# An expert product over two PSUM banks, and the first group's modes copied straight from SBUF to SBUF

## The chip, the cores and the metric

The kernel runs on one core of one Trainium2 chip. The metric is the device time of one execution in microseconds (us). The engines are TensorE (PE, its weight loads shown apart as PEld), VectorE (DVE), ScalarE (ACT), GpSimd (POOL) and SyncE (SP); SP and ACT also issue DMA transfers, shown as SPq and ACTq.

## The reference

The model is a Fourier neural operator over 32 images of 64x64 pixels, followed by one windowed attention and one mixture of experts. Cut to what matters here:

```python
# four layers; x is [B, 32, 64, 64], M1 = M2 = 20 modes kept
x_ft = jnp.fft.rfft2(x, norm='ortho')
out = jnp.einsum('bixy,ioxy->boxy', x_ft[:, :, :M1, :M2], w)   # per mode: 32 -> 32 channels
x1 = jnp.fft.irfft2(out_ft, s=(H, W), norm='ortho')            # back to pixels
x2 = jnp.einsum('bchw,oc->bohw', x, cw) + cb                   # pointwise
x = gelu(x1 + x2)
# ... fc1, gelu, fc2, attention over 65 tokens, and then the experts (64 of them, 6 chosen):
scores = softmax(top_logits)
xW = jnp.einsum('bsd,bskde->bske', x, lattice_weights[indices])
lattice_out = jnp.einsum('bske,bsk->bse', xW, scores)
```

## The kernel before, in words

**The layers.** The 32 images go in two passes of 16 (`GIMG`), each through four layers, so there are eight layers in all. A layer (`layer` in the PE part) has these steps. `forward`: a DFT over columns and rows; ACT copies its result (L1265) into `SPEC`, whose last axis holds 32 numbers per mode: real or imaginary part, and the image of the group and the group. `mix` (L1099 and L1107): per mode a product with the spectral weights; ACT copies the result from PSUM to `MIXED` in seven jobs (L1274, `mix_ready` counts them). `MIXED` has images and parts on partitions; the inverse needs modes on partitions, so the data must cross partitions, and that is done by DMA. `pointwise` (L1147, in layer 0 L1143), then `keep_busy(3)` (L1185), three dummy matmuls that stand ahead of the first inverse. `inverse_rows` (L1124) for group n = 0 to 3 of four images and half y = 0, 1, reading `MODE[n % 2]`; DVE transposes its result (L1367); `inverse_columns` (L1156) adds to the pointwise result in PSUM; ACT applies the Gelu (L1284).

**How the modes reach `MODE`.** For groups 1 to 3 SP stores 400 KB per group from `MIXED` into a DRAM scratch (`spec_scr`, L956), waits until it has landed, and loads it back in two transfers (`load_modes`, L940). For group 0, whose modes are wanted first, SP stores the first four of five column blocks d (80 KB each, L947) as soon as the mix job that holds them is done, waits for the four to land, loads them in two transfers (L940), and then waits for the whole mix. The fifth block goes by four direct copies from `MIXED` to `MODE[0]` of 20 KB each (`straight`, L277), two issued by SP behind those loads, two by ACT as soon as the seventh mix job is done. Only then does SP issue the three stores of groups 1 to 3. PE's first `inverse_rows` waits for the loads and for the four direct copies. In the first layer of the second pass SP waits, between the stores and the loads, until the hidden rows of the pass before have left (`ho_out`, their DMAs are L992), because `HO` shares memory with `MODE[0]`; ACT has the same wait ahead of its copies.

**The expert stage** (the tail, `tail_tensor` and `tail_vector`). The 2080 tokens go in five blocks z of 416 (`ZT`), and in each block over 64 experts, two to a step (32 steps `PAIRS` a block, n runs to 160). PE broadcasts the scores of step n over the partitions (`broadcast`, L443, bf16, into PSUM bank n % 4); DVE multiplies that bank by the tokens `YT` into `ZX` (L887); PE multiplies by the expert weights (`expert_products`, L453, two matmuls of 64 columns side by side for two values of n). PE's order is: broadcasts n and n+1, products n-4 and n-3. Broadcast n waits until DVE has freed its bank (product n-4). In between, at fixed steps, DVE adds the output projection (L870, steps `ADD_AT`), centres eight images (L704 to L706, `CENTRE_AT`) and finishes them (L711 to L880, `FINISH_AT`, with a square root on ACT in the middle); this happens for three of four parts inside the loop.

Of the kernel before, what the change touches and what calls it, by code (L numbers as in the profile page):

```python
# [6 lines left out]
NIMG, GRID, CH, MODES, LAYERS = 32, 64, 32, 20, 4  # L7
FC = 64
RI = 2
B4 = 4  # L10
NG = 4
GIMG = B4 * NG
# [4 lines left out]
KXD = MODES // B4  # L17
MIXB = KYG * KXD
KOUT = RI * MODES
# [13 lines left out]
LAST = MODES - B4  # L33
# [12 lines left out]
EH = EXPERTS // 2  # L46
# [5 lines left out]
NZ = 5  # L52
ZT = NT // NZ
# [7 lines left out]
PAIRS = EXPERTS // 2  # L61
# [4 lines left out]
ZR = 6  # L66
# [7 lines left out]
ALU = mybir.AluOpType  # L74
# [28 lines left out]
def vit_kernel(nc, coords_w, coords_c, expand0, fc0_t, tables, spec_w, fc1_w, fc1_b, fc2_w, fc2_b,  # L103
# [4 lines left out]
    with ctx:  # L108
# [3 lines left out]
        def sem(name):  # L112
            return ctx.enter_context(nc.semaphore(name))
# [63 lines left out]
        mix_full, mix_ready = Count(sem("mix_full"), N_MIX), Count(sem("mix_ready"), N_MIX)  # L177
        piece_used = Count(sem("weights_piece_used"), KYG, credit=KYG - 1)
        piece_in = [Count(sem(f"weights_piece_loaded{i}"), SLOT.count(i), unit=64) for i in range(RING)]
        stored = [Count(sem(f"modes_stored{g}"), 1, unit=16 if g else 16 * (KXD - 1)) for g in range(NG)]  # L180
        loaded_first, straight_in = Count(sem("first_modes_loaded"), 1, unit=32), Count(sem("last_modes_copied"), 1, unit=64)
        loaded = [None] + [Count(sem(f"modes_loaded{g}"), 1, unit=32) for g in range(1, NG)]
        ih_full, g_ready = Count(sem("inverse_rows_full"), 2 * NG), Count(sem("inverse_rows_ready"), 4 * NG, credit=4)
        x_full, x_ready = Count(sem("x_full"), 4 * NG, credit=16), Count(sem("x_ready"), 4 * NG, credit=16)
# [86 lines left out]
        SPR = [PSALL[:, 2 * i:2 * i + 2, 0:4 * TOK] for i in range(2)]  # L271
        PTP = PSALL[:, 4:6, 0:4 * TOK]

        def straight(eng, i):

            at = 64 * (i // 2) + RI * LAST
            eng.dma_start(MODE[0][at:at + RI * B4, i % 2].rearrange("p k o -> p (k o)"),  # L277
                          MIXED[NG * i:128:GIMG, LAST // B4 * MODES * CH:]).then_inc(straight_in.sem, 16)

        def tail_sync(sp):  # L280

# [11 lines left out]
        def tail_tensor(pe):  # L293
# [143 lines left out]
            def broadcast(n):  # L437
                z, ep = n // PAIRS, n % PAIRS
                if ep == 0:
                    pe.wait_ge(lo_ready, 2 * -(-(z + 1) * ZT // CT))  # L440
                if n >= 4:
                    pe.wait_ge(zx_ready, n - 3)
                pe.matmul(PS[n % 4][:, 0:ZT], SEL[:, ep % (EH // 2), :], PARTS3[2 * ep // EH][:, z * ZT:(z + 1) * ZT],  # L443
                          start=True, stop=True).then_inc(bc_full, 1)

            def expert_products(n):

                z, ep = n // PAIRS, n % PAIRS
                pe.wait_ge(zx_ready, n + 2)
                if ep == 0 and z >= 2:  # L450
                    pe.wait_ge(lt_ready, z - 1)
                for i in range(2):
                    m = pe.matmul(PS[4 + z % 2][64 * i:64 * i + GRID, 0:ZT], WE[:, ep + i, :], ZX[:, (n + i) % ZR, :],  # L453
                                  start=(ep == 0), stop=(ep == PAIRS - 2), tile_position=(0, 64 * i), skip_group_check=True)
                m.then_inc(zx_used, 1)
# [230 lines left out]
        def tail_vector(dve):  # L686
# [50 lines left out]
            def tail():  # L737
# [141 lines left out]
                    a = deviations(2, k)  # L879
                    nc.vector.tensor_tensor(TMP[:, a], TMP[:, a], over(st[:, 3, a]), ALU.mult).then_inc(ln_ready, 1)  # L880

                for n in range(NZ * PAIRS):
                    z = n // PAIRS
                    dve.wait_ge(bc_full, n + 1)
                    if n >= ZR and n % 2 == 0:
                        dve.wait_ge(zx_used, (n - ZR) // 2 + 1)
                    nc.vector.tensor_tensor(ZX[:, n % ZR, :], PS[n % 4][:, 0:ZT], YT[:, z * ZT:(z + 1) * ZT], ALU.mult  # L887
                                            ).then_inc(zx_ready, 1)
                    if n in ADD_AT:
                        add_projection(ADD_AT.index(n))  # L890
                    if n in CENTRE_AT:
                        centre_last(CENTRE_AT.index(n))
                    if n in FINISH_AT:
                        finish_last(FINISH_AT.index(n))
# [15 lines left out]
        def _(sp):  # L910
# [23 lines left out]
                                 spec_w[layer, kxd, j]  # L934
                                 ).then_inc(piece_in[slot].sem, 16)

            def load_modes(n, rows, count):

                for x in range(2):
                    sp.dma_start(MODE[n % 2][64 * x:64 * x + rows].rearrange("p y k o -> p y (k o)"),  # L940
                                 spec_scr[n].rearrange("x (s i) m -> (x s) i m", i=B4)[0:rows, 2 * x:2 * x + 2]).then_inc(count.sem, 16)

            def layer(p, l):

                for d in range(KXD - 1):
                    turn.wait(mix_ready, -(-(d + 1) * KYG // 4))
                    sp.dma_start(spec_scr[0, d], MIXED[0:128:NG, d * MODES * CH:(d + 1) * MODES * CH]).then_inc(stored[0].sem, 16)  # L947
                turn.wait(stored[0], 1)
                if l == 0 and p:
                    sp.wait_ge(ho_out.sem, p * ho_out.stride)  # L950
                load_modes(0, RI * LAST, loaded_first)
                turn.wait(mix_ready, N_MIX)
                for i in range(2):
                    straight(sp, i)
                for n in range(1, NG):
                    sp.dma_start(spec_scr[n].rearrange("x j m -> j x m"),  # L956
                                 MIXED[n:128:NG].rearrange("j (x m) -> j x m", x=KXD)).then_inc(stored[n].sem, 16)
                for n in range(1, NG):
                    turn.wait(stored[n], 1)
                    if n >= 2:  # L960
                        turn.wait(ih_full, 2 * (n - 1))
                    load_modes(n, KOUT, loaded[n])

            def load_pieces(l):
                for kxd in range(RING):
# [34 lines left out]
        def _(pe):  # L1000
# [111 lines left out]
            def inverse_rows(l, n, y):  # L1112
                if n == 0 and y == 0:
                    turn.wait(mix_ready, N_MIX)
                    turn.wait(loaded_first, 1)
                    turn.wait(straight_in, 1)
                elif y == 0:
                    turn.wait(loaded[n], 1)
                if n or y:
                    turn.wait(g_ready, 4 * n + 2 * y)  # L1120
                for a, b in ((0, 8), (8, MODES // 2)):
                    for z in range(2):
                        for x in range(2):
                            m = pe.matmul(PSALL[64 * z:64 * z + 64, 4 + 2 * x + a // 8, 0:(b - a) * 2 * CH],  # L1124
                                          TABLES[64 * x:64 * x + 64, l, EH0 + 64 * z:EH0 + 64 * z + 64],
                                          MODE[n % 2][64 * x:64 * x + 64, y, a:b, :],
                                          start=True, stop=True, tile_position=(64 * x, 64 * z))
                m.then_inc(ih_full.sem, 1)
# [130 lines left out]
        def _(act):  # L1259
# [3 lines left out]
            def spectrum(r, banks):  # L1263
                turn.wait(sp_full, r + 1)
                nc.scalar.copy(  # L1265
                    SPEC[:].rearrange("p k x (r i n) -> p n i (k x) r", r=RI, n=NG)[:, r // 2, 2 * (r % 2):2 * (r % 2) + 2],
                    banks[r % 2][:, 0:2 * SPW].rearrange("p (b n r) -> p b n r", b=2, r=RI)
                ).then_inc(sp_ready.sem, 1)

            def mixed(p, l):  # L1270
# [5 lines left out]
                turn.wait(mix_ready, N_MIX)  # L1276
                if l == 0 and p:
                    act.wait_ge(ho_out.sem, p * ho_out.stride)
                for i in range(2, B4):
                    straight(act, i)  # L1280

            def activated(l, n, t, p):
                turn.wait(x_full, 4 * n + 2 * t + p + 1)
# [269 lines left out]
```

## Time and profile before

| | us |
|---|---|
| median of 3 runs | 1193.69 |
| lowest, highest | 1191.68, 1194.4 |
| profiled execution, its own time | 1191.19 |
| its span in the trace | 1189.3 |
| PE busy | 1079.4 (91%) |
| DVE busy | 631.0 (53%) |
| ACT busy | 418.0 (35%) |
| mean granted clock of TensorE | 0.957 |

The span is the part of the execution that the trace covers; 1.9 us of the execution's own time lie around it. Times in the rows are from the span's start. A clock of 1.00 is 2.4 GHz and 0.50 is 1.2 GHz.

### The profile page before, as it was taken

To read this page: it belongs to the slowest core of one execution; us is meant where nothing else is said; L and a number is where in the kernel's file an instruction comes from. 1 tells how busy PE (TensorE), PEld (TensorE's weight loads), DVE (VectorE), ACT (ScalarE), POOL (GpSimd) and SP (SyncE) were. 2 spreads that over 40 slices of the span, in tenths; PEclk is the share of its full clock that TensorE was granted. 3 is DMA by queue.
4 is the path that set the end of the run, shared out by engine and by line. 5 is a ranking of instruction groups with operands and counts; after the bars stand their busy time and mean duration, and the time that the engine had idled before them with its cause. 6 is when DMAs were issued, how large, how long until landed. Compare 5 with 4: busy or idle time off the path is not lost.

```text
span 1189.3 us, 34374 instructions
## 1 busy us (share of the span) xinstructions
PE 1079.4 (91%) x15860; PEld 719.4 (60%) x15860; DVE 631.0 (53%) x870; ACT 418.0 (35%) x586; POOL 126.7 (11%) x120
## 2 busy tenths in 40 slices
PE   4899899989999998999899899989999999549996
PEld 3577677757866633777578667757326888422221
DVE  2248335823844221358238445824154676778887
ACT  2332223123222485232232223123676775360000
POOL 6000000000000000000000000010011754162111
PEclk9899989999999999899999999999899999559998
DMA  5220130022012301300220040020001000000000
GB/s 178 96 71 2 61 92 16 2 96 71 2 43 72 125 6 56 98 19 2 96 71 2 30 123 16 2 96 16 4 22 39 2 1 2 1 1 1 5 5 10
DMA packets 24629, 49.25 MB, mean 41 GB/s; under 512 B 9821, under 2 KB 10872, under 8 KB 23845
## 3 DMA queue, kind: packets, MB, share of 16 engines
q1 hardware_dynamic: 23798, 46.44, 12.4%
q8 instruction: 125, 2.05, 0.7%
q0 software_dynamic: 432, 0.29, 0.1%
q10 hardware_dynamic: 256, 0.33, 0.1%
q14 instruction: 18, 0.15, 0.0%
HBM read 32.87 MB, written 13.51 MB: 39 GB/s over the span
## 4 chain that ended last, share of the span: by engine, by line
PE 75%; DVE 12%; DMA 4%; ACT 3%; issue 2%; SPq 1%; POOL 1%; POOLq 0%; DVEq 0%
PE PSALL L1156 22%; PE PSALL L1014 9%; PE PSALL L1124 7%; PE PSALL L1031 7%; DVE WORK L1348 5%; PE PSALL L453 5%; PE PSALL L1234 4%; PE PSALL L1147 4%; PE PSALL L1099 3%; PE PSALL L1244 3%; PE PSALL L443 2%; PE PSALL L380 2%; DMA spec_scr<-MIXED 2%; DVE WORK L1367 1%; PE PSALL L1143 1%
## 5 line engine op out<-in xcount | busy, mean ns | idle before, releaser
L1367 DVE STREAM_TRANSPOSE WORK<-PSALL 128x1024 f32<-128x1024 f32 x128 | 152.4, 1229 | 333.8 <-PE PSALL L1124 333.8
L1156 PEld LDWEIGHTS PSALL<-EW,WORK 64*128 64x128 f32 x4096 | 255.5, 197 | 64.4 <-issue 48.8
L1156 PE MATMUL PSALL<-EW,WORK 64*128 64x128 f32 x4096 | 271.2, 287 | 12.1 <-DVE WORK L1367 12.1
L1284 ACT ACTIVATE X<-PSALL,TABLES 128x1024 f32<-128x1024 f32 x128 | 141.7, 1113 | 350.3 <-PE PSALL L1156 350.3
L1348 DVE STREAM_TRANSPOSE WORK<-PSALL 128x1024 f32<-128x1024 f32 x100 | 119.1, 1229 | 58.0 <-PE PSALL L1014 54.2
L1031 PE MATMUL PSALL<-TABLES,WORK 128*128 128x128 f32 x1000 | 136.4, 285 | 5.1 <-DVE WORK L1348 0.8
L1031 PEld LDWEIGHTS PSALL<-TABLES,WORK 128*128 128x128 f32 x1000 | 118.7, 191 | 32.3 <-issue 18.3
L1265 ACT COPY SPEC<-PSALL 128x400 f32<-128x400 f32 x64 | 53.4, 843 | 175.7 <-PE PSALL L1031 172.5
L1014 PE MATMUL PSALL<-WORK,DW 32*64 32x256 f32 x3200 | 103.0, 388 | 12.6 <-DMA B<-in_fc_b 12.6
L1344 DVE STREAM_TRANSPOSE WORK<-X 128x1024 f32<-128x1024 f32 x96 | 111.4, 1204 | 0.0
L887 DVE TENSOR_TENSOR WORK<-PSALL,X 128x416 f32<-128x416 f32 x160 | 85.3, 582 | 15.2 <-PE PSALL L443 15.2
L1014 PEld LDWEIGHTS PSALL<-WORK,DW 32*64 32x64 f32 x3200 | 67.3, 131 | 31.3 <-issue 13.5
L609 POOL MEMSET SW<- 64x4160 f32 x1 | 3.6, 3559 | 762.2 <-PE PSALL L1107 762.2
L1318 ACT ACTIVATE WORK<-PSALL,B 128x1024 f32<-128x1024 f32 x64 | 67.9, 1110 | 18.8 <-PE PSALL L1234 18.5
L453 PE MATMUL PSALL<-WORK,SPEC 128*64 128x416 f32 x320 | 74.5, 546 | 0.0
L1411 DVE TENSOR_SCALAR WORK<-PSALL,B 128x512 f32<-128x512 f32 x32 | 23.9, 749 | 79.5 <-PE PSALL L1244 60.8
L1147 PE MATMUL PSALL<-X,TABLES 32*32 32x512 f32 x1536 | 59.7, 599 | 0.2 <-ACT X L1284 0.2
L1124 PE MATMUL PSALL<-WORK,TABLES 64*64 64x128 f32 (+1 forms) x512 | 46.8, 484 | 13.8 <-DMA WORK<-MIXED 13.8
L1234 PE MATMUL PSALL<-X,W 32*64 32x512 f32 x512 | 52.5, 636 | 4.4 <-ACT X L1284 2.4
L1099 PE MATMUL PSALL<-SW,SPEC 128*32 128x128 f32 x1600 | 49.2, 275 | 7.3 <-ACT SPEC L1265 6.4
L1099 PEld LDWEIGHTS PSALL<-SW,SPEC 128*32 128x32 f32 x1600 | 41.9, 109 | 13.7 <-ACT SPEC L1265 7.9
L443 PE MATMUL PSALL<-SW 128*128 128x416 bf16 x160 | 44.4, 354 | 3.7 <-DVE WORK L887 3.3
(141 smaller groups left out, 983.7 us busy)
## 6 DMA issues: line engine op xcount, KB each, us to landing
SW<-in_spec_w SPq DMA_DIRECT2D x160, 80.0 KB, 2.4
spec_scr<-MIXED SPq DMA_DIRECT2D x24, 400.0 KB, 3.2
SPEC<-spec_scr SPq DMA_DIRECT2D x32, 200.0 KB
WORK<-spec_scr SPq DMA_DIRECT2D x16, 200.0 KB
spec_scr<-MIXED SPq DMA_DIRECT2D x32, 80.0 KB, 1.8
WORK<-spec_scr SPq DMA_DIRECT2D x16, 160.0 KB, 2.6
WORK<-in_coords_w SPq DMA_DIRECT2D x2, 1024.0 KB, 4.8
XC<-in_coords_c SPq DMA_DIRECT2D x2, 1024.0 KB, 7.1
```

The costliest lines, as they stand in the source:

```text
L453: m = pe.matmul(PS[4 + z % 2][64 * i:64 * i + GRID, 0:ZT], WE[:, ep + i, :], ZX[:, (n + i) % ZR, :], start=(ep == 0), stop=(ep == PAIRS - ...
L1014: m = pe.matmul(banks[p][64 * j:64 * j + 64, 256 * i:256 * i + 256], DW[Q * p:Q * p + Q, h, :], pixels[Q * p:Q * p + Q, i, h, 4 * j:4 * j ...
L1031: m = pe.matmul(bank[:, at + kyg * KOUT:at + kyg * KOUT + 128], z[:, 2 * kyg:2 * kyg + 2].rearrange("p y c v -> p (y c v)"), TABLES[:, l, ...
L1099: m = pe.matmul(mix_bank[job % 2][32 * q:32 * q + RI * GIMG, (blk % 4) * 128:(blk % 4 + 1) * 128], SPEC[:, kyg, 4 * kxd + q, :], pieces[SL ...
L1124: m = pe.matmul(PSALL[64 * z:64 * z + 64, 4 + 2 * x + a // 8, 0:(b - a) * 2 * CH], TABLES[64 * x:64 * x + 64, l, EH0 + 64 * z:EH0 + 64 * z ...
L1147: pe.matmul(bank[col, :], TABLES[row, l, 0:CH], X[row, n, :, q, 2 * t:2 * t + 2, :].rearrange("p b c w -> p b (c w)"), start=True, stop=Tr ...
L1156: m = pe.matmul(PS[2 * p + z][:, 2 * b * GRID:(2 * b + 2) * GRID], G[64 * z:64 * z + 64, n % 2, b, h:h + 4, :, c].rearrange("p q o -> p (q ...
L1234: m = pe.matmul(PS[4 + d][FC * j:FC * (j + 1), :], W1[Q * d:Q * d + Q, :], X[Q * d:Q * d + Q, m0 // B4, m0 % B4, 2 * j:2 * j + 2].rearrang ...
L1284: nc.scalar.activation(X[:, n].rearrange("p b (z d) c w -> p d z b (c w)", z=2)[:, p, :, :, 2 * t * GRID:2 * (t + 1) * GRID], PSALL[:, 2 * ...
L1344: nc.vector.transpose(XP[:, k % 4].rearrange("p h u c v -> p (h u) v c"), X[:, n, b].rearrange("p q c (h w) -> p h (q c) w", h=2)).then_in ...
L1348: return nc.vector.transpose(z.rearrange("p y c v -> p c y v"), PSALL[:, bank:bank + 4, 256 * b:256 * b + 256].rearrange("p k (c g) -> p c ...
L1367: nc.vector.transpose(G[:, n % 2, 2 * x + y].rearrange("p h o v -> p o h v"), PSALL[:, 4 + 2 * x:6 + 2 * x, :].rearrange("p k (h o v) -> p ...
```

## The change

Two parts. In the expert stage one VectorE instruction multiplies two PSUM banks (steps n and n+1) by the same tokens; the counters `bc_full` and `zx_ready` count pairs, and the waits on both engines follow. For the modes, the images of a group are numbered in another order inside `SPEC` (y before x), so that one strided slice of `MIXED` holds both images y of one x; the five blocks of group 0 then all go by `straight`, two copies of 40 KB each (x = 0, 1), eight of them on SP as their mix jobs finish and two on ACT. Group 0's store, its landing wait and its loads go away. The loads of groups 1 to 3 read the same bytes in pieces of half the length. The wait for `ho_out` on SP moves ahead of the first copy.

```diff
-        stored = [Count(sem(f"modes_stored{g}"), 1, unit=16 if g else 16 * (KXD - 1)) for g in range(NG)]
-        loaded_first, straight_in = Count(sem("first_modes_loaded"), 1, unit=32), Count(sem("last_modes_copied"), 1, unit=64)
+        stored = [Count(sem(f"modes_stored{g}"), 1, unit=16) for g in range(NG)]
+        straight_in = Count(sem("first_modes_copied"), 1, unit=16 * 2 * KXD)
...
-        def straight(eng, i):
+        def straight(eng, d, x):
 
-            at = 64 * (i // 2) + RI * LAST
-            eng.dma_start(MODE[0][at:at + RI * B4, i % 2].rearrange("p k o -> p (k o)"),
-                          MIXED[NG * i:128:GIMG, LAST // B4 * MODES * CH:]).then_inc(straight_in.sem, 16)
+            at = 64 * x + RI * B4 * d
+            eng.dma_start(MODE[0][at:at + RI * B4].rearrange("p y k o -> p y (k o)"),
+                          MIXED[NG * x:128:2 * NG, d * MODES * CH:(d + 1) * MODES * CH]
+                          ).then_inc(straight_in.sem, 16)
...
-                if n >= 4:
-                    pe.wait_ge(zx_ready, n - 3)
-                pe.matmul(PS[n % 4][:, 0:ZT], SEL[:, ep % (EH // 2), :], PARTS3[2 * ep // EH][:, z * ZT:(z + 1) * ZT],
-                          start=True, stop=True).then_inc(bc_full, 1)
+                if n >= 4 and n % 2 == 0:
+                    pe.wait_ge(zx_ready, n // 2 - 1)
+                m = pe.matmul(PS[n % 4][:, 0:ZT], SEL[:, ep % (EH // 2), :], PARTS3[2 * ep // EH][:, z * ZT:(z + 1) * ZT],
+                              start=True, stop=True)
+                if n % 2:
+                    m.then_inc(bc_full, 1)
...
-                pe.wait_ge(zx_ready, n + 2)
+                pe.wait_ge(zx_ready, n // 2 + 1)
...
-                for n in range(NZ * PAIRS):
+                for n in range(0, NZ * PAIRS, 2):
                     z = n // PAIRS
-                    dve.wait_ge(bc_full, n + 1)
-                    if n >= ZR and n % 2 == 0:
+                    dve.wait_ge(bc_full, n // 2 + 1)
+                    if n >= ZR:
                         dve.wait_ge(zx_used, (n - ZR) // 2 + 1)
-                    nc.vector.tensor_tensor(ZX[:, n % ZR, :], PS[n % 4][:, 0:ZT], YT[:, z * ZT:(z + 1) * ZT], ALU.mult
+                    nc.vector.tensor_tensor(ZX[:, n % ZR:n % ZR + 2, :], PSALL[:, n % 4:n % 4 + 2, 0:ZT],
+                                            YT[:, z * ZT:(z + 1) * ZT].unsqueeze(1).broadcast_to([128, 2, ZT]), ALU.mult
                                             ).then_inc(zx_ready, 1)
...
-            def load_modes(n, rows, count):
+            def load_modes(n, count):
 
                 for x in range(2):
-                    sp.dma_start(MODE[n % 2][64 * x:64 * x + rows].rearrange("p y k o -> p y (k o)"),
-                                 spec_scr[n].rearrange("x (s i) m -> (x s) i m", i=B4)[0:rows, 2 * x:2 * x + 2]).then_inc(count.sem, 16)
+                    sp.dma_start(MODE[n % 2][64 * x:64 * x + KOUT].rearrange("p y k o -> p y (k o)"),
+                                 spec_scr[n].rearrange("d (s y x) m -> (d s) x y m", y=2, x=2)[:, x]).then_inc(count.sem, 16)
 
             def layer(p, l):
 
+                if l == 0 and p:
+                    sp.wait_ge(ho_out.sem, p * ho_out.stride)
                 for d in range(KXD - 1):
                     turn.wait(mix_ready, -(-(d + 1) * KYG // 4))
-                    sp.dma_start(spec_scr[0, d], MIXED[0:128:NG, d * MODES * CH:(d + 1) * MODES * CH]).then_inc(stored[0].sem, 16)
-                turn.wait(stored[0], 1)
-                if l == 0 and p:
-                    sp.wait_ge(ho_out.sem, p * ho_out.stride)
-                load_modes(0, RI * LAST, loaded_first)
+                    for x in range(2):
+                        straight(sp, d, x)
                 turn.wait(mix_ready, N_MIX)
-                for i in range(2):
-                    straight(sp, i)
...
-                    turn.wait(loaded_first, 1)
                     turn.wait(straight_in, 1)
...
-                    SPEC[:].rearrange("p k x (r i n) -> p n i (k x) r", r=RI, n=NG)[:, r // 2, 2 * (r % 2):2 * (r % 2) + 2],
+                    SPEC[:].rearrange("p k m (r y x n) -> p n x y (k m) r", r=RI, x=2, n=NG)[:, r // 2, r % 2],
...
-                for i in range(2, B4):
-                    straight(act, i)
+                for x in range(2):
+                    straight(act, KXD - 1, x)
```

## Rows read from the trace of the kernel before

**Rows 1.** The page: granted clock of TensorE in 40 slices of the span

```profile
PEclk9899989999999999899999999999899999559998
```

**Rows 2.** Waits: waiter, released by: us in total, times, longest

```profile
PE PSALL L1124 <- DMA WORK<-MIXED: 13.8, 8, 2.1
```

**Rows 3.** Timeline, layer 1, pass 0: start, duration, instructions, [idle before, releaser]

```profile
136.67 3.46 SPq L947 DMA_DIRECT2D spec_scr<-MIXED  x4
...
139.87 0.80 ACT L1274 COPY MIXED<-PSALL 128x512 f32<-128x512 f32 x2 [0.22 <-PE PSALL L1099]
...
140.70 1.18 ACTq L277 DMA_DIRECT2D WORK<-MIXED  x2
...
141.35 2.84 PE L1185 MATMUL PSALL<-WORK,ident 128*128 128x512 f32 x6
...
142.25 0.78 SPq L940 DMA_DIRECT2D WORK<-spec_scr  x2
...
143.48 1.28 SPq L277 DMA_DIRECT2D WORK<-MIXED  x2
144.81 1.96 SPq L956 DMA_DIRECT2D spec_scr<-MIXED  x3
...
146.28 1.31 PE L1124 MATMUL PSALL<-WORK,TABLES 64*64 64x512 f32 x16 [2.09 <-DMA WORK<-MIXED]
...
148.95 2.08 PE L1156 MATMUL PSALL<-EW,WORK 64*128 64x128 f32 x16 [1.36 <-DVE WORK L1367]
...
157.21 1.09 PE L1124 MATMUL PSALL<-SPEC,TABLES 64*64 64x512 f32 x8
```

**Rows 4.** Busy time by stretch, same layer: PE, PEld, DVE, ACT, POOL, clock, DMA share, GB/s

```profile
150.00:152.00 2.00, 2.00 (x18) 1.17 (x20) 0.03 (x1) 0.00 (x0) 0.00 (x0) 0.50 0.46 164
```

**Rows 5.** Timeline, first inverses: the first of the eight layers, and the last

```profile
40.83 1.31 PE L1124 MATMUL PSALL<-WORK,TABLES 64*64 64x512 f32 x16 [2.01 <-DMA WORK<-MIXED]
...
51.60 1.31 PE L1124 MATMUL PSALL<-SPEC,TABLES 64*64 64x512 f32 x16
...
786.92 1.31 PE L1124 MATMUL PSALL<-WORK,TABLES 64*64 64x512 f32 x16 [1.79 <-DMA WORK<-MIXED]
...
795.69 1.31 PE L1124 MATMUL PSALL<-SPEC,TABLES 64*64 64x512 f32 x16
```

**Rows 6.** Source line L277: issue time of one in ns, min/median/max

```profile
L277 ACTq DMA_DIRECT2D WORK<-MIXED x16: 570/572/1153, 35.3 to 782.3; - x16
```

**Rows 7.** Timeline, second pass, layer 0: the last hidden rows' DMAs

```profile
462.20 2.38 SPq L992 DMA_DIRECT2D hid_scr<-WORK  x8
```

**Rows 8.** Page: DMA issues of the stores: KB each, us from issue to landing

```profile
spec_scr<-MIXED SPq DMA_DIRECT2D x24, 400.0 KB, 3.2
```

**Rows 9.** Timeline, expert stage, one steady step

```profile
1087.23 0.53 PE L443 MATMUL PSALL<-SW 128*128 128x416 bf16 x2
1087.62 1.09 DVE L887 TENSOR_TENSOR WORK<-PSALL,X 128x416 f32<-128x416 f32 x2 [0.22 <-PE PSALL L443]
...
1087.69 0.92 PE L453 MATMUL PSALL<-WORK,SPEC 128*64 128x416 f32 x4
...
1088.54 0.52 PE L443 MATMUL PSALL<-SW 128*128 128x416 bf16 x2
```

**Rows 10.** Timeline, expert stage: after a centring, after a finish, and the last products

```profile
1119.61 0.82 PE L443 MATMUL PSALL<-SW 128*128 128x416 bf16 x2
...
1120.36 0.92 PE L453 MATMUL PSALL<-WORK,SPEC 128*64 128x416 f32 x4
...
1125.05 0.35 PE L443 MATMUL PSALL<-SW 128*128 128x416 bf16 x1 [0.88 <-DVE WORK L887]
...
1175.81 2.32 PE L453 MATMUL PSALL<-WORK,SPEC 128*64 128x416 f32 x12
```

**Rows 11.** Groups by form: line, form, count | busy, mean ns of one | idle before

```profile
L887 DVE TENSOR_TENSOR WORK<-PSALL,X 128x416 f32<-128x416 f32 x160 | 85.3, 582 | 15.2 <-PE PSALL L443 15.2
...
L781 DVE TENSOR_TENSOR SW<-PSALL,BAND 65x520 f32<-65x520 f32 x32 | 22.1, 689 | 21.2 <-PE PSALL L359 21.2
```

More of the change, by code:

```diff
@@ L961, in layer @@
                         turn.wait(ih_full, 2 * (n - 1))
-                    load_modes(n, KOUT, loaded[n])
+                    load_modes(n, loaded[n])
             def load_pieces(l):
```

## The prediction

> **What bounds the kernel now.** I read the page first, then the waits, then timelines of the two places that the change touches, and last the clock by stretches. TensorE is busy for 91% of the span, so a microsecond counts only if TensorE gets it back, as idle time or as clock. The clock is at full speed in most slices and drops now and then in the layers, and for long only ahead of the expert stage [rows 1]. The table of waits has one line on TensorE that this change addresses: eight times, once a layer, the first inverse waits for a DMA into WORK, 13.8 us in all, 2.1 at most [rows 2].
>
> The timeline of one layer shows where that comes from [rows 3]. The mix is finished and copied at 140.67. TensorE then runs the pointwise part and the dummy matmuls until 144.19. On the DMA side SP has stored four blocks, and because their landing has to be awaited its loads go out at 142.25, its two direct copies from 143.48 to 144.76, and TensorE starts at 146.28: 2.09 us idle. So what ends last is not ACT's pair of copies (issued by 141.88) but SP's pair, which stands in SP's queue behind a round trip through DRAM. From the end of the second issue to TensorE's start there are 1.52 us; I use that as the landing time of such a copy.
>
> There is a second loss behind the first. After the inverse TensorE has another gap, 1.36 us, for the transpose on VectorE [rows 3]; then the granted clock falls to its lower level, 1.2 GHz, and the column matmuls and the next inverse run at half speed [rows 4]. From the first inverse's start to the start of the next group's inverse this layer takes 157.21 - 146.28 = 10.93 us. The last layer takes 795.69 - 786.92 = 8.77, the first one 51.60 - 40.83 = 10.77 [rows 5]. Over all eight layers (the first and the last are shown) the values are 10.77, 10.93, 10.35, 8.77, 10.95, 10.33, 8.77, 8.77; the three at 8.77 kept 2.4 GHz. Against 8.77 the other five lost 2.00 + 2.16 + 1.58 + 2.18 + 1.56 = 9.5 us. In the last layer the clock held in spite of 1.79 us idle and the 1.36 us gap after it.
>
> The expert stage repeats every 1088.54 - 1087.23 = 1.31 us for a step of two [rows 9]. VectorE works 1.09 of that and waits 0.22 for TensorE; TensorE does not wait. It is TensorE's stage.
>
> **The change part by part.** Profiled execution: 1191.19 us, span 1189.3.
>
> *The direct copies.* SP now issues two copies per block instead of a store. One copy's issue took 0.57 us on ACT (median) and 1.15 at most [rows 6], 0.64 on SP (1.28 for two) [rows 3]. Nearest to the new form, a strided SBUF slice into SBUF, are just these; it moves 40 KB instead of 20, so I take 0.64 for SP and keep 0.45 and 1.15 as ends. In the layer of rows 3 SP may start at 136.67 (the second mix job): eight issues take 5.1 us, no block is ready much later than SP comes to it, so they end by about 141.9; plus 1.5, the last lands at 143.4. ACT issues its two from 140.70 to 141.88 as before and they land at 143.4. For the double size I add 0.1: 143.5, against 144.19 at which the dummy matmuls end. The wait is then over before TensorE asks, with 0.7 us to spare, and what is next on TensorE is its own work. Gain: the 13.8 us of idle [rows 2]. At 0.45 an issue nothing changes; at 1.15 the eight end at 145.9, the last lands at 147.4, and TensorE waits 3.2 us instead of 2.1.
>
> In the first layer of the second pass SP waits first for the hidden rows, whose last DMA is issued at 464.58 [rows 7]; with 1.5 us of landing SP starts at 466.1 instead of 464.9, ends at 471.2, and the data is there at 472.7, where the dummy matmuls end at 472.4. That layer keeps up to 0.3 us of its wait. ACT has the same wait, but comes to it at 468.9.
>
> Moved and added transfers: SP's three stores of 400 KB go out some 2.9 us earlier (141.9 instead of 144.8), behind SP's eight copies and beside ACT's two. Group 1's load follows them, and is wanted only at 157.21, so the finer pieces of the loads are covered by about ten microseconds; groups 2 and 3 are loaded a group ahead, with more cover still. The copy into SPEC has the same shape with another stride, and the mix reads 32 adjacent numbers as before: nothing.
>
> The Trainium skill, "DMA: Bandwidth & Descriptors", section "Queues, rings and completion order", speaks against this part: each DMA engine takes packets from its queues in turn, and a completion's write lands only after every earlier write of that engine, across its queues. By that ACT's pair could complete behind SP's big stores; what that would cost is the second rival.
>
> *The clock.* With the wait gone, one gap of 1.36 us is left where there were two. In three layers both gaps together left the clock at full speed (the last layer's first one was 1.79 us [rows 5]), so the second alone should too. I take all of the 9.5 us; the other end is none of it. The same skill's "TensorE: Matmul & The Clock Gate", "Why this matters for your kernels", warns only of single idle gaps longer than any here. By that page these drops would not come from the gaps, and would stay: that is the third rival. The rows bear it out poorly: all five drops came right behind this pair of gaps.
>
> *The expert stage.* A product over two banks: the 416-element form takes 582 ns; a form over 520 elements in two banks, also with a repeated operand, takes 689 [rows 11], so 1.03 ns an element, and 832 elements take 582 + 416 x 1.03 = 1010 ns. The upper end is two singles, 1164. VectorE saves 80 x (1.09 - 1.01) = 6 us of busy time, which stands beside TensorE's and is worth nothing. The pair starts after the second broadcast, and its result is wanted one full step later, so the steady step stays 1.31 us, up to the upper end. TensorE's own gaps in it (from the broadcasts' start to the products' 0.46, then 0.85, of which the products alone take 0.70 where three steps stand together, 2.32 us for 12 records [rows 10]) lie at the switch between the two kinds of matmul. At the end of the loop the waits are there and the gaps are not, so I give the removed waits nothing; at the very most 80 x 0.25 = 20 us.
>
> TensorE stands still after VectorE's other work. After a centring the distance from broadcast to product is 0.75 us instead of 0.46, after a finish the second broadcast waits 0.88 and the first product comes 1.05 late in all [rows 10]: 1.34 a part, 4.0 for three. Now both products of a step are done before VectorE turns away. The next one starts one product later (0.43) and is twice as long (0.43), but is wanted 1.31 - 0.18 = 1.13 later: 0.27 less each time. The centring's stall goes, the finish's shrinks to some 0.85 to 0.95: 0.4 a part, 1.2 in all. At the loop's start the fifth broadcast waits for a pair instead of one product: +0.3. Sum -0.9, with ends -4 and +1.
>
> Sum: -13.8 + 0.2 (the one layer) - 9.5 - 0.9 = -24.0, so 1167.2 on the profiled execution. That one is 2.5 us below the median of the runs. If the others are longer because more layers lost the clock, as one more layer costs 1.6 to 2.2 us, this goes away too (1167); if not, 1169.7. I say 1168.
>
> **The rivals.**
> 1. *The wait comes back in another place (slower).* Eight issues in a row on SP replace four; where one takes 1.15 us, as ACT's slowest did [rows 6], TensorE waits 1.1 us longer than now in each layer, and the three clean layers lose the clock as well: 8 x 1.1 + 3 x 2.1 = +15, less 0.9: 1205. It decides when an issue takes over 1.01 us: then eight end at 144.76 as now. For it: SP has no slack of its own. Against: SP's own pair took 0.64 each.
> 2. *ACT's pair lands behind the stores.* The first store, issued at 141.9, takes 3.2 us to its landing [rows 8], so ACT's pair would be there at 145.1: TensorE waits 0.9 instead of 2.1. That is 7 us of the gain lost, the clock still held (a smaller sum of gaps than in the last layer): 1174. For it: they start together. Against: now SP's second copy also has the stores at its heels (144.81) and lands 1.5 us later.
> 3. *The clock drops all the same.* 1167.2 + 9.5 = 1176.7; with half of the drops 1172.
> 4. *No copy lands earlier*, because DMA engines carry all ten late: 1190.
> 5. *The double product opens TensorE's step*: were the pair slower than 1.31 us, 80 steps would each grow; at twice the single time it is not.
>
> **How the numbers follow.** Forecast 0.64; rival 2 0.10; rival 3 0.14; rival 4 0.04; rival 1 0.05; rival 5 with anything else that takes all of the gain 0.03. The clock also drops at two places in the tail and is released there at moments that will shift with the 24 us; each is worth up to 2 us either way, so the forecast's own range is 1164 to 1172. The range takes in rivals 2 and 3: 1162 to 1179. A difference under 0.2% (2.4 us) can't be told from none. Faster: the forecast, 2, 3 and most of 5: 0.92; same 0.03; slower 0.05.
>
> **What would show it.** Right: the wait of the first inverse for WORK<-MIXED gone from the table or under 1 us in all; ten L277-like issues a layer of about 0.6 us; eight spans from inverse to inverse of 8.8 us at clock 1.00; 80 products of about 1010 ns, and a step of 1.31 us. Wrong: an idle time of over 0.5 us before the first inverse, a clock of 0.5 in the first 10 us after it, a step that is longer or clearly shorter than 1.31.

## The result, and the profile after

The changed kernel takes 1177.17 us (median of 4 runs, 1174.05 to 1179.14); the kernel before, with a fourth run taken beside it, 1194.05. The ratio is 0.9847, 95% interval 0.9802 to 0.9893. A second set of runs (e10 below) gave 0.9883 (0.9854 to 0.9911), so the gain is 1.2 to 1.5%. The forecast was 1168, with a range of 1162 to 1179: the direction is right and the time inside the range, near its upper end, but the forecast itself is 9 us too low. The profiled execution takes 1177.26 us, its span is 1175.4, that is 13.9 us less than before, where 24.0 were reckoned.

The table of waits, and the timeline of TensorE and of the DMA queues in the third layer (where the copies went as planned):

```profile
PE PSALL L1124 <- DMA WORK<-MIXED: 5.6, 8, 1.6
```

```profile
237.32 5.33 SPq L277 DMA_DIRECT2D WORK<-MIXED  x8
...
241.34 1.30 ACTq L277 DMA_DIRECT2D WORK<-MIXED  x2
...
242.00 2.84 PE L1185 MATMUL PSALL<-WORK,ident 128*128 128x512 f32 x6
...
242.69 1.95 SPq L957 DMA_DIRECT2D spec_scr<-MIXED  x3
...
245.09 1.31 PE L1124 MATMUL PSALL<-WORK,TABLES 64*64 64x512 f32 x16 [0.26 <-DMA WORK<-MIXED]
...
247.77 1.21 PE L1156 MATMUL PSALL<-EW,WORK 64*128 64x128 f32 x16 [1.36 <-DVE WORK L1367]
...
253.86 1.31 PE L1124 MATMUL PSALL<-SPEC,TABLES 64*64 64x512 f32 x16
```

The wait for the first group's modes fell from 13.8 us [rows 2] to 5.6; it did not go. The dummy matmuls end at 244.84 and the inverse starts 0.26 later. From there to the next group's inverse it is 253.86 - 245.09 = 8.77 us, at full clock, where the layer of [rows 3] took 10.93. All eight idle times and spans after: 1.58, 1.16, 0.26, 0.29, 0.94, 0.89, 0.26, 0.26 us of idle, and 8.77 in every layer but the fifth, which took 10.42 after an idle time of 0.94: its clock fell.

```profile
468.00:470.00 2.00, 2.00 (x18) 1.17 (x20) 0.23 (x1) 0.00 (x0) 0.00 (x0) 0.50 0.37 117
```

That is the fifth layer's row of busy time by stretch, with a clock of 0.50 like [rows 4]. The spans sum to 71.8 us instead of 79.6. So the copies brought 13.8 - 5.6 = 8.2 us of waiting and 7.8 us of clock, 16.0 together.

The chain of waits (start, duration, what) shows the end of the copies, first in the third layer and then in the second:

```profile
241.38 0.61 SPq L277
...
242.03 2.93 DMA WORK<-MIXED
```

```profile
138.23 1.59 SPq L277
...
140.26 0.62 SPq L277
...
140.93 2.41 DMA WORK<-MIXED
```

The last issue starts at 242.03 and the data is there 2.93 us later; before, that was 1.98 us, 144.17 to 146.15, by the same view. This time, from the start of the last issue to the end of the wait, is called the landing below. TensorE's inverse starts 0.09 to 0.14 us after it. In the second layer one single issue took 1.59 us instead of 0.61, and TensorE waited 1.16. There ACT's last copy had been issued 1.4 us before SP's, and the landing is 2.41; in the third layer the two were issued at the same moment.

The first layer is another case. ACT's first copy took 1.52 us to issue, so SP issued its first store at 37.25, ahead of ACT's second copy at 37.44:

```profile
35.88 1.52 ACTq L277
...
37.44 3.38 DMA WORK<-MIXED
```

The landing is 3.38 us, the longest of the eight, and TensorE waited 1.58.

In the expert stage one product of 832 elements takes 1021 ns, and the steady step is the same as in [rows 9], 1096.54 - 1095.23 = 1.31 us:

```profile
L890 DVE TENSOR_TENSOR WORK<-PSALL,X 128x832 f32<-128x832 f32 x80 | 80.7, 1021 | 19.7 <-PE PSALL L444 19.4
```

```profile
1095.23 0.53 PE L444 MATMUL PSALL<-SW 128*128 128x416 bf16 x2
...
1095.80 1.02 DVE L890 TENSOR_TENSOR WORK<-PSALL,X 128x832 f32<-128x832 f32 x1 [0.28 <-PE PSALL L444]
...
1096.54 0.53 PE L444 MATMUL PSALL<-SW 128*128 128x416 bf16 x2
...
1112.96 0.53 PE L444 MATMUL PSALL<-SW 128*128 128x416 bf16 x2 [0.80 <-DVE WORK L890]
```

After a finish TensorE waits 0.80 us (the last row), three times, and the step is 0.86 longer than usual, where it was 1.05 [rows 10]; after a centring the broadcasts are 1.47 us apart instead of 1.31, 0.16 more, where it was 0.29.

### The profile page after: what moved, and what is told of

Read it like the earlier page. It is cut to its first block, busy times and chain, and to the rows that moved or that the text cites. A ratio compares the mean times of both kernels' runs of the same rounds, so it can differ in the third digit from the quotient of the medians.

```text
span 1175.4 us, 34294 instructions
## 1 busy us (share of the span) xinstructions
PE 1072.6 (91%) x15860; PEld 713.8 (61%) x15860; DVE 626.4 (53%) x790; ACT 418.9 (36%) x586; POOL 126.7 (11%) x120
## 4 chain that ended last, share of the span: by engine, by line
PE 76%; DVE 12%; ACT 4%; DMA 2%; issue 2%; SPq 1%; POOL 1%; ACTq 0%; POOLq 0%; DVEq 0%
PE PSALL L1156 22%; PE PSALL L1015 9%; PE PSALL L1124 7%; PE PSALL L1032 7%; PE PSALL L456 5%; DVE WORK L1348 5%; PE PSALL L1234 4%; PE PSALL L1147 4%; PE PSALL L1100 4%; PE PSALL L1244 3%; PE PSALL L444 3%; PE PSALL L381 2%; DMA WORK<-MIXED 2%; DVE WORK L1367 2%; PE PSALL L360 2%
## 5 line engine op out<-in xcount | busy, mean ns | idle before, releaser
L1156 PEld LDWEIGHTS PSALL<-EW,WORK 64*128 64x128 f32 x4096 | 250.6, 193 | 65.5 <-issue 48.3
L1156 PE MATMUL PSALL<-EW,WORK 64*128 64x128 f32 x4096 | 266.8, 283 | 12.8 <-DVE WORK L1367 12.8
L890 DVE TENSOR_TENSOR WORK<-PSALL,X 128x832 f32<-128x832 f32 x80 | 80.7, 1021 | 19.7 <-PE PSALL L444 19.4
L1015 PEld LDWEIGHTS PSALL<-WORK,DW 32*64 32x64 f32 x3200 | 67.2, 131 | 31.5 <-issue 13.6
L1124 PE MATMUL PSALL<-WORK,TABLES 64*64 64x128 f32 (+1 forms) x512 | 42.7, 449 | 5.6 <-DMA WORK<-MIXED 5.6
```

The lines of the kernel that those rows point to most:

```text
L1015: m = pe.matmul(banks[p][64 * j:64 * j + 64, 256 * i:256 * i + 256], DW[Q * p:Q * p + Q, h, :], pixels[Q * p:Q * p + Q, i, h, 4 * j:4 * j ...
L1156: m = pe.matmul(PS[2 * p + z][:, 2 * b * GRID:(2 * b + 2) * GRID], G[64 * z:64 * z + 64, n % 2, b, h:h + 4, :, c].rearrange("p q o -> p (q ...
```

## The experiments

Each was run beside the kernel before; a ratio is to that kernel on the same chip. The experiments e6, e7 and e9 leave out part of the data and were run once each, so only their traces are read, not their times. "Idle" is the sum over eight layers of the wait of the first inverse, "spans" the sum from first inverse to next group's inverse (before: 13.8 and 79.6; changed: 5.6 and 71.8).

**e1, the expert part alone**

```diff
 # kernel before, with the expert stage's hunks of the change and no others
+ nc.vector.tensor_tensor(ZX[:, n % ZR:n % ZR + 2, :], PSALL[:, n % 4:n % 4 + 2, 0:ZT], ...)
```

> Only the expert part of the change (one VectorE product over two banks); the modes go as before. If the copies carry the whole gain: from the first to the last expert product 111.3 to 111.8 us (111.77 before, 111.36 with the whole change), TensorE's steady step still 1.31 us, the eight waits of the first inverse still 13 to 14 us in all, ratio to before 0.997 to 1.002. Rival: the expert part carries a share of the 14 us that the changed trace shows; then ratio 0.995 or less, and the step shorter than 1.31 us.

Ratio 1.0017 (0.9991 to 1.0043): no difference. Idle 14.3, spans 77.3 (four layers lost the clock). From first to last expert product 110.7 us, a little below what was expected, step 1.31. **The expert part carries none of the gain that can be measured.** Seen over all traces, from the first broadcast to the last product, it is worth about 1 us: 115.0 to 115.6 us in the four traces with single products (before, e2, e4, e5), 114.1 to 114.8 in the ten with double ones.

**e2, the copies alone**

```diff
 # the change, without the expert stage's hunks
```

> Only the copies part; the expert stage as before. If the copies carry the whole gain: the waits of the first inverse 5 to 6 us in all, the eight spans from the first inverse to the next group's inverse 70 to 74 us in all (79.6 before), ratio 0.982 to 0.989. Rival (expert part shares the gain): ratio above 0.990.

Ratio 0.9893 (0.9861 to 0.9924), a little above what was expected; idle 5.1, spans 71.7. The idle time and the spans are those of the whole change. With e1 this settles which part works.

**e3, the big stores after the copies have landed**

```diff
                 turn.wait(mix_ready, N_MIX)
+                turn.wait(straight_in, 1)
                 for n in range(1, NG):
                     sp.dma_start(spec_scr[n]...
```

> The whole change, but SP waits for all ten copies to land before it issues the stores of groups 1 to 3. The changed trace has 2.9 us from the start of the last copy's issue to the inverse, where the kernel before had 2.0. Theory A, the stores right behind the copies hold them up: then 2.9 becomes 2.0, the wait goes in the five layers without a slow issue, in all 1 to 2.5 us instead of 5.6, and the time falls by 2 to 4 us against the whole change (ratio to before 0.980 to 0.984). Theory B, the copy's own size and shape (40 KB, two pieces an engine) or the eight copies ahead of it: 2.9 stays, waits 5 to 6 us in all, ratio 0.985 as for the whole change. The stores come some 2.5 us later, which the group 1 inverse (8.8 us after the first) still covers.

Ratio 0.9862 (0.9827 to 0.9897). Idle 4.6, and 0.30 to 0.40 in the four layers without a slow issue. The chain of waits there, in the third layer:

```profile
239.80 0.65 ACTq L277
...
240.48 2.98 DMA WORK<-MIXED
```

Theory B, in seven of the eight layers: with no store anywhere near, the last copies still need 3.0 us where SP and ACT issue them together. In the first layer it was theory A. There ACT's first issue was as slow as in the change (1.52 us), but no store went ahead of the second, and the landing fell from 3.38 to 2.42:

```profile
36.99 2.42 DMA WORK<-MIXED
```

The wait there fell from 1.58 to 0.65 us, and that is nearly all of the 1.0 us by which the idle sum is lower. The three traces of the copies without this edit agree on the first layer: 1.58, 1.50 (e2) and 1.57 (e10).

**e4, seven dummy matmuls in the kernel before**

```diff
-                keep_busy(3)
+                keep_busy(7)
```

> The kernel before with seven dummy matmuls instead of three ahead of the first inverse: 4 x 0.43 = 1.7 us more dummy work a layer, which fills the wait for the DMA (1.5 to 2.1 us) and adds up to 0.2 us where the wait was shorter. Nothing else moves. If the clock drops come from this idle time: all eight spans from first inverse to next inverse become 8.8 us (70 in all instead of 79.6), a gain of 8 to 9.5 us, ratio 0.992 to 0.995, with the inverse starting no earlier. Rival: the drops have another cause (the DMA burst, or the second gap of 1.36 us alone): then five or so of the spans stay at 10.3 to 10.9 us and the ratio is 1.000 to 1.001.

Ratio 1.0037 (1.0015 to 1.0058): slower, against both theories. I had read the dummies wrong. The row below has 14 records for 7 matmuls: each has two, and a dummy costs 0.85 us, not 0.43: (6.28 - 2.84) / 4 = 0.86, with the row of three in [rows 3].

```profile
140.69 6.28 PE L1185 MATMUL PSALL<-WORK,ident 128*128 128x512 f32 x14
```

So four more dummies moved the inverse back by 3.4 us less the wait that they filled, 1.3 to 1.9 us a layer, some 13 us in all. The spans were 8.8 in all eight layers, 70.3 us: the 9.3 us of clock did come back, and less than they cost.

**e5, five dummies, the amount that fits**

```diff
-                keep_busy(3)
+                keep_busy(5)
```

> The kernel before with five dummy matmuls ahead of the first inverse instead of three. The run with seven showed that one costs 0.85 us (kernel trace: four more moved the inverse's possible start by 3.4 us), not the 0.43 that had been reckoned, so two more add 1.7 us, about the wait that is there (1.5 to 2.1 us). If the clock drops come from the idle time ahead of the first inverse: all eight spans 8.8 us (70.2 in all), the inverse's start at most 0.2 us later than before, time 7 to 9 us less than before, ratio 0.992 to 0.995. Rival (the dummy work only hides a wait, the drops are chance): spans as before, ratio 1.000 to 1.001.

Ratio 0.9945 (0.9924 to 0.9967). Idle 1.0, spans 70.2 with none above 8.84. The second layer, with the inverse 0.28 us after the dummies and its successor 8.77 after it:

```profile
144.13 1.31 PE L1124 MATMUL PSALL<-WORK,TABLES 64*64 64x512 f32 x16 [0.28 <-DMA WORK<-MIXED]
...
152.90 1.31 PE L1124 MATMUL PSALL<-SPEC,TABLES 64*64 64x512 f32 x16
```

**The clock drops came from the idle time ahead of the inverse.** Work of no use in its place, with the data no earlier, gives back 6 us. In the spans it is 9.4; the dummies themselves outlast the wait in some layers, and the rest of the difference was not followed. The other traces fit: over all fourteen, the clock dropped behind the first inverse in 17 of the 53 layers with 0.5 us or more of this idle time, and in none of the 59 with less. The length alone does not decide it: 0.52 us lost the clock once (e12), 1.79 kept it [rows 5].

**e6, only the copies of the last two blocks** (the modes of the other three are left out)

```diff
-                    for x in range(2):
+                    for x in range(2 if d == KXD - 2 else 0):
                         straight(sp, d, x)
```

> The whole change without the six copies of the first three blocks (their part of the modes is left out): SP issues only the two of the fourth block, at the fifth mix job, ACT the two of the fifth. From ACT's second issue to the inverse the changed trace has 2.9 us at the least. If the queue of eight copies (or SP's pair going out at the same moment as ACT's) makes that long: 2.0 us, as for one copy before, and no wait in any layer. If a copy of 40 KB itself takes so long to land: 2.9 us from ACT's second issue, a wait of 0.2 to 0.3 us in each layer without a slow issue, as with the whole change.

Neither. SP was now free at the end of the mix and issued its stores at 244.89, between ACT's two copies, and the data came later than ever:

```profile
244.41 0.64 ACTq L277
...
245.09 3.43 DMA WORK<-MIXED
```

Idle 6.6, three layers lost the clock. The stores were issued 0.2 to 0.9 us ahead of ACT's second copy in seven layers, and there the landing was 3.43 to 3.70 us. In the sixth layer the first store went out 0.05 us after ACT's second copy, and the inverse started 2.77 us after that copy's issue, with no wait. With a store ahead it started 3.56 to 3.84 us after it. So a store issued ahead of the last copy costs 0.8 us or more (e9 gives the same comparison without stores); in the changed kernel SP's own copies kept the stores back in all layers but the first.

**e7, every copy cut to half** (one image of each pair is left out)

```diff
-            eng.dma_start(MODE[0][at:at + RI * B4]...,   MIXED[NG * x:128:2 * NG, ...])
+            eng.dma_start(MODE[0][at:at + RI * B4, 0]..., MIXED[NG * x:128:GIMG, ...])
```

> The whole change with every one of the ten copies cut to half, 20 KB: 8 source partitions into 8, the shape of the copies before; the other image of each pair is left out. If size and shape make the landing long: 2.0 us from the last issue's start to the inverse's data, so no wait in layers without a slow issue. If it is the number of copies in flight: 2.7 to 2.9 us stay and a wait of 0.1 to 0.3 us a layer.

Idle 1.5, nearly all in the first two layers, which had a slow issue (the sixth had one too and waited 0.05). In the second layer the last copy needs 2.66 us, not 2.0:

```profile
138.56 0.59 SPq L277
...
139.20 2.66 DMA WORK<-MIXED
```

In the fifth and sixth layer the inverse starts 2.44 us after the last issue; the layers with 40 KB and the same distance to ACT's last copy (0.4 to 0.5 us) have 2.87 to 3.06. So size is one part of the 2.9 and not all of it.

**e8, three queues**

```diff
-                    for x in range(2):
+                    for x in range(2 if d < KXD - 2 else 0):
                         straight(sp, d, x)
                 turn.wait(mix_ready, N_MIX)
+                straight(sp, KXD - 1, 0)      # ACT: straight(act, KXD - 1, 1)
...
+                    turn.wait(mix_ready, -(-(KXD - 1) * KYG // 4))      # GpSimd
+                    for x in range(2):
+                        straight(pool, KXD - 2, x, pool_in)
```

> The whole change with the copies on three queues: blocks 0 to 2 on SP, block 3 on GpSimd, of block 4 one copy on SP and one on ACT. SP's last copy then starts to issue where the mix ends and not 0.65 us later, behind it the stores come 0.6 us earlier. If the wait left over is that of the queues: last issue starts 0.6 us earlier, the wait goes in the layers without a slow issue and shrinks by 0.6 in the others, 1 to 3 us in all instead of 5.6; time 2 to 4 us below the whole change, ratio to before 0.980 to 0.984. Rival: GpSimd's copies land later than SP's did (its issue costs 1 us or more each) and the wait stays at 5 us or grows; ratio 0.986 or more.

Ratio 0.9807 (0.9786 to 0.9828), 1170.0 us. Idle practically none, spans 70.3: better than the whole change, and the first kernel in which both losses are gone. Timeline of its fourth layer:

```profile
335.71 4.71 SPq L278 DMA_DIRECT2D WORK<-MIXED  x7
...
338.99 1.12 POOL L278 DMA_DIRECT2D WORK<-MIXED  x2 [100.39 <-ACT MIXED L1277]
...
339.75 0.62 ACTq L278 DMA_DIRECT2D WORK<-MIXED  x1
...
340.40 2.84 PE L1188 MATMUL PSALL<-WORK,ident 128*128 128x512 f32 x6
...
343.17 1.31 PE L1127 MATMUL PSALL<-WORK,TABLES 64*64 64x512 f32 x16
...
351.94 1.31 PE L1127 MATMUL PSALL<-SPEC,TABLES 64*64 64x512 f32 x16
```

The last issues start at the end of the mix, and the inverse follows the dummies without a gap. One issue on SP took 1.72 us in this trace, and its layer waited 0.15.

**e9, e6 with the stores after the landing** (same modes left out)

```diff
 # e6, and
+                turn.wait(straight_in, 1)     # ahead of the stores
```

> As e6 (six of the ten copies left out, with their part of the modes), and the stores of groups 1 to 3 wait until the four copies have landed. In e6 the data came 3.5 us after ACT's second issue, with the stores issued at the same moment; in e3, with all ten copies and late stores, 3.0 us after the last issue. If the stores caused e6's 3.5 and the eight earlier copies e3's 3.0, both gone give 2.0 to 2.2 us and no wait. If a pair of 40 KB copies needs it by itself: 2.8 to 3.0 us and a wait of 0.2 to 0.3 us in each layer.

Idle 0.45 in the first layer, 0.15 in the second and none after it. Without a wait the trace gives only an upper end: the inverse starts 2.74 to 2.77 us after ACT's second issue. The two landings that can be read are 2.41 (first layer) and 2.84 (second). Against e6, which differs only in the stores, the inverse comes 0.8 us sooner or more, and 1.3 us sooner in the first layer. Whether a pair needs 2.8 us by itself stays open: SP's last copy went out 0.9 us before ACT's here, so the two queues did not end together.

**e10, the whole change once more:** no edit.

> The whole change once more, for a comparison with e11 on one chip. Ratio to before 0.984 to 0.990, waits of the first inverse 4.5 to 6 us in all; how many of its layers lose the clock is chance (0 to 2).

1176.51 us, 0.9883 (0.9854 to 0.9911), idle 6.0, one layer of 10.15.

**e11, three queues and one dummy less**

```diff
-                keep_busy(3)
+                keep_busy(2)
```

> Three queues as in e8, with two dummy matmuls instead of three. If the copies land well ahead of the third dummy's end: up to 0.85 us less a layer, 3 to 6 us in all, ratio to before 0.976 to 0.979. If they land just at its end (in e8 one layer waited 0.15 us): the 0.85 us come back as a wait, and the time is that of e8 (0.981), or worse by 1.6 to 2.2 us a layer where the clock drops.

1170.8 us, 0.9833 (0.9798 to 0.9869), on the chip of e10. The waits are back (0.37 to 1.05, 5.1 in all) in place of the 6.8 us of dummies; its runs spread from 1164 to 1177. Not told apart from e8.

**e12, no copies on ACT**

```diff
-                straight(act, KXD - 1, 1)     # ACT; SP issues both copies of block 4
-                    for x in range(2 if d < KXD - 2 else 0):
+                    for x in range(2 if d < KXD - 3 else 0):     # GpSimd: blocks 2 and 3
```

> As e11 (three queues, two dummies), but ACT issues no copy: blocks 0 and 1 on SP, 2 and 3 on GpSimd, both copies of block 4 on SP behind the end of the mix. The last issue then starts 0.65 us later than in e11. In e11 the data came 2.9 us after the last issue (SP's and ACT's side by side), in the kernel before 2.0 us after SP's last one. If it is two queues issuing side by side that makes the landing long: 2.0 us again, the waits 0.2 us a layer (e11: 0.38 to 1.05) and the time 1 to 2 us below e11. If each 40 KB copy needs 2.7 to 2.9 us whoever issues it: waits 1.0 to 1.2 us in every layer, some 8 to 9 us in all, and the time 3 to 5 us above e11 (ratio to before 0.986 to 0.988).

Ratio 0.9805 (0.9779 to 0.9832), 1169.8 us, idle 5.4, spans 71.8 (one layer lost the clock). The chain, in six of eight layers the same to 0.01 us:

```profile
238.19 0.61 SPq L278
...
238.84 2.36 DMA WORK<-MIXED
```

Between the two again, and this takes the 2.9 apart: 20 KB with one queue at the end 1.98 (kernel before), 40 KB with one queue 2.36, 40 KB with SP and ACT at the same moment 2.9. **About 0.4 us go with the size, 0.55 with two queues ending side by side.** The kernels with ten copies on SP and ACT say the same of the second part (the change, e2, e3, e10, no store ahead): with the last copies of the two queues issued at most 0.1 us apart the landing is 2.91 to 3.09 us, at 0.4 to 0.5 it is 2.73 to 2.92, at 0.9 to 1.0 it is 2.42 to 2.71, and from 1.1 on 2.37 to 2.56. What does not fit are this kernel's second and sixth layer: 2.91 and 2.94 us with only SP issuing at the end. That stays open.

Its time equals e8's. Both lie below e10 by more than the intervals; the interval of the first set of runs of the change (0.9802 to 0.9893) overlaps theirs.

## Why the prediction was right, and where it was not

- *What bounds the kernel, and which wait ends last:* right. The wait was that of [rows 2], e2 shows that its removal is the gain, and e1 that nothing else is.
- *The clock as the second half of the loss:* right, and shown by e5. Of 9.5 us 7.8 came; the rest stayed in the fifth layer, where 0.94 us of idle were left. The third rival, that the drops have another cause, is out. The step behind it, that the gap of 1.36 us alone keeps the clock, holds in all 59 layers whose first gap was under 0.5 us. By the rule of the Trainium skill ("TensorE: Matmul & The Clock Gate", "Why this matters for your kernels") only single idle gaps longer than any here are warned of, and by it the drops would not come from these; here gaps of 1.5 to 2.1 and 1.36 us with 1.3 us of work between them cost up to 2.2 us a time, and the measurement decides.
- *Issue times:* 0.61 us against the 0.64 taken, and eight issues took 5.3 us against 5.1. What the median hid were slow ones: in this trace three layers had an issue of 1.5 to 1.6 us (the first on ACT, the second and sixth on SP). The row with the maximum of 1153 ns [rows 6] was a hint; I used it as the price of every issue, in a rival, and not as the price of one in each few layers. The idle times of these layers are 1.3, 0.9 and 0.6 us above the undisturbed ones: 2.8 us of the 5.6. Of the first layer's 1.3 only 0.4 is the slow issue itself; 0.9 is the store that it let go ahead (e3).
- *The landing, the term that failed:* the prediction has a copy land 1.5 us after its issue and adds 0.1 for the double size. It took this from the end of the issue to TensorE's start, so 1.6 us; in the third layer it is 245.09 - 242.64 = 2.45, 0.8 more. The 1.5 us of the row before belonged to a small copy, issued when ACT's were 2.2 us old or more; size costs about 0.4, and two queues ending together 0.55 (e12 against e3 and e11). With the eight issues, 0.1 to 0.2 us longer than reckoned, that is about 1.0 us, where 0.7 us was the spare time. Hence the 0.26 to 0.29 us in the undisturbed layers, and a wait in all eight.
- *ACT's pair behind the stores (second rival):* it came true in one layer of eight, the first, where a slow issue on ACT let SP's first store go ahead of ACT's second copy, and cost 0.9 us there (e3). In the other seven the stores' issue started after the last copy's, and nothing shows that it cost anything. e6 shows it in seven layers, at 0.8 us or more.
- *The second pass's first layer:* up to 0.3 us of wait was reckoned, 0.94 came, and 0.94 or 0.97 in e3 and e10 too, mostly from the same landing (2.66 us here).
- *The expert stage:* right. Product 1010 reckoned, 1021 measured; step unchanged; the stalls of 1.34 us a part became 1.02, three times, where 0.4 less was reckoned; the start cost 0.28 (first broadcast to first product 3.48 us instead of 3.20). That would make -0.7. It is -0.1 in this trace, because the low clock reached 8.5 us into the stage instead of 6.9. The -0.9 is below what runs can tell.
- *The tail's clock:* 1.6 us the wrong way. From the last layer to the expert stage the trace after is longer, and more than all of it is in the attention's scores: from the first use of a score (L781, after L784) to the last 85.4 us instead of 82.8, at a clock that was low for 6.8 us instead of 3.4. In the other traces it is 82.8 (eight of them) or 85.1 to 85.3 (four), with the copies and without them. That was put at up to 2 us either way, and I take it for chance.

In numbers: -8.2 for the wait instead of -13.6, -7.8 for the clock instead of -9.5, -0.1 in this trace for the experts instead of -0.9, +0.7 ahead of and between the layers, +1.6 in the rest of the tail: -13.9 before rounding. Of the 10 us that are missing some 5.4 are the wait and 1.7 the clock that went with it; the +0.7 and the +1.6 were in no sum. That the time still fell inside the range is owed to the range, which was drawn to take in rivals 2 and 3.

## What to carry to other kernels

Take a transfer's landing time from a row in which as much is in flight as there will be, and ask whether the row's copy was alone; compare the spare time that is left with that doubt, not with the median. A short wait of TensorE can cost as much again in clock: compare the same stretch in repetitions with and without the drop, and prove it with dummy work of the same length. Where the last transfers have to wait for the last producer, bring all others to other queues, so that the last issue is not behind them, and let no large store be issued ahead of it.

## What the runs showed of the hardware that was not expected

- An SBUF to SBUF copy of 20 KB by one queue has landed 1.98 us after the start of its issue, one of 40 KB 2.36, and 40 KB beside another queue's copy 2.9 to 3.1, with or without 400 KB stores behind it (in two layers of e12 also without the other queue's copy). With the first of the stores issued 0.2 to 0.9 us ahead of it, on the other queue, it is 3.3 to 3.7.
- Single issues of such copies take 1.0 to 1.8 us instead of 0.6, in one to three of eight layers, on SP or ACT, in every trace but e12's. On SP they go with transfers that look like the fetching of instructions: of all 208 SP issues longer than 0.95 us between 25 and 830 us in the fourteen traces, 196 end 0.35 to 0.41 us after the end of a transfer of 16384 bytes on the queue that the profile lists as "q8 instruction"; of the 4005 shorter issues 41 do. In the second layer of the change that transfer ends at 139.41 and the slow issue at 139.81. No experiment moved one of the two to see the other move. On ACT the slow one is the first copy that ACT issues, 1.14 to 1.55 us in all thirteen traces that have one; that cause stays open.
- The load from DRAM in pieces of 2560 bytes instead of 5120 takes 0.74 to 0.76 us to issue instead of 0.31 to 0.33 (medians). It was hidden here.
- The copies on GpSimd took 0.56 us each to issue (median), against 0.61 on SP and 0.62 on ACT, and landed in time.
- A dummy fp32 matmul of 128x128 by 512 is two records and 0.85 us.
